# Combining-weight rows spread over partitions from on-chip memory instead of from a stored copy, and the loading loop written out

## What is computed

```python
probs = jax.nn.sigmoid(x @ router_w.T + expert_bias[None, :])
top_w, top_idx = jax.lax.top_k(probs, 8)
top_w = top_w / (jnp.sum(top_w, -1, keepdims=True) + 1e-9) * 2.5
combine = jnp.zeros((T, 160)).at[jnp.arange(T)[:, None], top_idx].set(top_w)
h1 = jax.nn.silu(jnp.einsum('th,eih->eti', x, w_gate))     # 160 experts, 64 wide
h1w = h1 * combine.T[:, :, None]
routed = jnp.einsum('eti,ehi->th', h1w, w_down)
```

## Time and profile before

| what | value |
|---|---|
| time before, median of 3 runs (lowest to highest) | 978.6 us (977.95 to 981.06) |
| the profiled execution: its own time, its span | 979.47 us, 977.4 us |
| granted TensorE clock, mean over the span | 0.997 of full |
| busy share of the span: PE, DVE, ACT, POOL | 96%, 79%, 70%, 41% |
| bytes moved by DMA, mean rate | 160.57 MB, 164 GB/s |
| HBM read, written | 105.60 MB, 2.42 MB |

### The profile page before, as it was taken

How to read it: one execution, slowest core, us unless ns; L and a number is a source line. 1 busy time by engine, 2 the same in 40 slices (tenths; PEclk the granted TensorE clock), 3 DMA queues, 4 the chain that set the end, 5 groups by cost and what they waited for, 6 DMA issues and landing times.

```text
span 977.4 us, 15761 instructions
## 1 busy us (share of the span) xinstructions
PE 940.8 (96%) x4592; PEld 684.4 (70%) x4592; DVE 770.3 (79%) x1450; ACT 681.3 (70%) x1171; POOL 402.8 (41%) x265
## 2 busy tenths in 40 slices
PE   4899999999999999999997999999999999999997
PEld 2656666666666666666543888888888888888886
DVE  5866766766676676676764999999999999999996
ACT  4656666666666666666655777877777777777775
POOL 0688888898888888898900000000000000000000
PEclk9999999999999999999999999999999999999999
DMA  7957644544553563454105999999999999999992
GB/s 217 235 161 202 166 115 103 130 100 117 130 122 78 125 152 92 104 130 101 47 18 139 224 221 220 220 219 220 218 218 220 217 219 217 221 216 220 219 218 61
DMA packets 71633, 160.57 MB, mean 164 GB/s; under 512 B 10416, under 2 KB 36336, under 8 KB 61856
## 3 DMA queue, kind: packets, MB, share of 16 engines
q1 hardware_dynamic: 70816, 158.66, 72.8%
q10 hardware_dynamic: 768, 1.31, 0.4%
HBM read 105.60 MB, written 2.42 MB: 111 GB/s over the span
## 4 chain that ended last, share of the span: by engine, by line
PE 88%; DVE 5%; ACT 3%; issue 2%; DMA 1%; POOL 1%; ACTq 0%; SPq 0%; DVEq 0%
PE ps L635 44%; PE ps L439 11%; PE ps L426 11%; PE ps L415 5%; PE ps L417 5%; PE ps L389 5%; PE ps L452 2%; PE ps L400 2%; ACT prob L729 1%; DVE prob L1032 1%; POOL prob L904 1%; DMA strips<-comb_rows 0%; DVE PT L208 0%; PE ps L374 0%; PE ps L485 0%
## 5 line engine op out<-in xcount | busy, mean ns | idle before, releaser
L904 POOL TENSOR_SCALAR prob<-prob,rinv 128x512 f32<-128x512 f32 x256 | 398.1, 1568 | 87.8 <-DVE rinv L1049 85.7
L729 ACT ACTIVATE prob<-prob,nmax 128x512 f32<-128x512 f32 x256 | 183.0, 716 | 138.7 <-DVE nmax L1032 138.6
L635 PE MATMUL ps<-hT,wT 128*128 128x512 f32 x960 | 243.9, 390 | 1.3 <-ACT oT L820 1.3
L1235 DVE TENSOR_TENSOR PT<-v_sb,strips 128x1024 f32<-128x1024 f32 x160 | 196.1, 1225 | 44.0 <-ACT v_sb L871 33.6
L871 ACT ACTIVATE v_sb<-ps 128x1024 f32<-128x1024 f32 x160 | 164.6, 1029 | 90.2 <-PE ps L635 89.9
L635 PEld LDWEIGHTS ps<-hT,wT 128*128 128x128 f32 x960 | 180.4, 188 | 40.5 <-issue 3.0
L635 PE MATMUL ps<-stack,wT 128*128 128x512 f32 x640 | 197.8, 391 | 4.3 <-DVE wT L1222 4.3
L208 DVE COPY PT<-ps 128x512 f32<-128x512 f32 x128 | 88.4, 691 | 135.4 <-PE ps L426 133.0
L1222 DVE TENSOR_TENSOR wT<-PT,stack 128x1024 fp32r<-128x1024 f32 x160 | 195.0, 1219 | 0.0
L863 ACT CAST stack<-PT 128x1024 fp32r<-128x1024 f32 x160 | 166.6, 1041 | 2.9 <-DVE PT L1235 2.9
L426 PEld LDWEIGHTS ps<-ident,prob 128*128 128x128 f32 x1024 | 114.4, 141 | 74.5 <-POOL prob L904 51.0
(11 more groups left out here) (113 smaller groups left out, 726.8 us busy)
## 6 DMA issues: line engine op xcount, KB each, us to landing
strips<-comb_rows SPq DMA_DIRECT2D x152, 512.0 KB, 12.8
stack<-qk SPq DMA_DIRECT2D x128, 256.0 KB, 3.8
k_low<-qk SPq DMA_DIRECT2D x64, 128.0 KB, 3.8
hT<-qk SPq DMA_DIRECT2D x64, 128.0 KB, 3.7
strips<-bias_rows SPq DMA_DIRECT2D x8, 896.0 KB, 5.6
strips<-in_L_ffn_w_gate SPq DMA_DIRECT2D x80, 64.0 KB, 11.2
strips<-in_L_ffn_w_down SPq DMA_DIRECT2D x80, 64.0 KB, 12.9
strips<-comb_rows SPq DMA_DIRECT2D x16, 256.0 KB, 5.7
```

The source lines that it names most:

```text
L635: last = nc.tensor.matmul(ps[:, bank + c, :], weights(a), rows(m, c), start=start and k == 0, stop=stop and k == 2, skip_group_check=True)
L729: nc.scalar.activation(prob[:, u, :], prob[:, u, :], ACT.Exp, bias=nmax[:, u:u + 1], scale=-1.0, accum_out=rsum[:, u:u + 1]).then_inc(s_ex ...
L904: nc.gpsimd.tensor_scalar(prob[:, u, :], prob[:, u, :], rinv[:, u:u + 1], None, ALU.mult).then_inc(s_prob, 1)
L1235: nc.vector.tensor_tensor(weighted[:, k % 4, :], silu[:, k % 2, :], cb[:, r, half * HALF:(half + 1) * HALF], ALU.mult).then_inc(s_mul, 1)
```

## The change

The DRAM tensor `comb_rows`, its stores and their semaphores are gone. Each row load takes its row straight from the one partition of `combT` or `combT2` that holds it, with a step of zero over the 64 destination partitions. SP waits for the copies into these tensors (`s_cev`) where it waited for the stores. The partition of the source can no longer be computed in a loop, so the loop on SP's queue is a Python loop now, and its 19 turns stand one after the other in SP's program.

```diff
-    comb_rows = nc.dram_tensor("comb_rows", [EPAIRS, 2, T], F32, kind="Internal").ap()
...
-        s_cst = [sem(f"comb_stored{b}") for b in range(B)]
...
                 for half in range(2):
-                    row = comb_rows[bass.ds(i * DEPTH + r, 1), half, tokens]
-                    sp.dma_start(cb[half * I:(half + 1) * I, r, tokens], row.broadcast_to(
-                        [I, tokens.stop - tokens.start])).then_inc(loaded or s_cb[r], 16)
+                    expert = 2 * (i * DEPTH + r) + half
+                    row = combT[expert:expert + 1, tokens] if expert < P else combT2[expert - P:expert - P + 1, tokens]
+                    count = tokens.stop - tokens.start
+                    spread = bass.AP(row.tensor, row.offset, [list(row.ap[0]), [0, I], [1, count]])
+                    sp.dma_start(cb[half * I:(half + 1) * I, r, tokens].rearrange("p (o n) -> p o n", o=1), spread.rearrange("o p n -> o p n")).then_inc(loaded or s_cb[r], 16)
...
-            sp.wait_ge(s_cst[0], 32)
-            sp.wait_ge(s_cst[1], 32)
+            sp.wait_ge(s_cev, 4)
             for r in range(2):
                 load_rows(0, r, slice(0, HALF), s_first_rows[r])
-            sp.wait_ge(s_cst[2], 32)
-            sp.wait_ge(s_cst[3], 32)
+            sp.wait_ge(s_cev, 8)
...
-            with sp.Fori(0, EPAIRS // DEPTH - 1) as i:
+            for i in range(EPAIRS // DEPTH - 1):
...
-            def store_comb(b):
-                act.wait_ge(s_cev, 2 * (b + 1))
-                act.dma_start(flat[0:P, b * S:(b + 1) * S], combT[:, b * S:(b + 1) * S]).then_inc(s_cst[b], 16)
-                act.dma_start(flat[P:E, b * S:(b + 1) * S], combT2[:, b * S:(b + 1) * S]).then_inc(s_cst[b], 16)
```

More of the change, by code:

```diff
@@ L808, in copy_comb @@
                 nc.scalar.copy(combT2[:, b * S:(b + 1) * S], ps[0:E - P, COMBS + 1, :]).then_inc(s_cev, 1)
-            flat = comb_rows.rearrange("n two t -> (n two) t")
-            def store_comb(b):
-                act.wait_ge(s_cev, 2 * (b + 1))
-                act.dma_start(flat[0:P, b * S:(b + 1) * S], combT[:, b * S:(b + 1) * S]).then_inc(s_cst[b], 16)
-                act.dma_start(flat[P:E, b * S:(b + 1) * S], combT2[:, b * S:(b + 1) * S]).then_inc(s_cst[b], 16)
             def shared_silu(n):
@@ L842, in _ @@
             copy_comb(0)
-            store_comb(0)
             sigmoids(2)
@@ L854, in _ @@
             copy_comb(1)
-            store_comb(1)
             shared_silu(0)
@@ L874, in round_of @@
                         copy_comb(3)
-                        store_comb(3)
                     if not (first and k == 0):
@@ L882, in _ @@
             copy_comb(2)
-            store_comb(2)
             shared_silu(2)
```

## The result

The changed kernel takes 3,560.8 us (median of 4 runs, 3,560.0 to 3,563.1) against 978.6 us before, a ratio of 3.63 with a 95% interval from 3.617 to 3.643. The forecast was 3,585 us. The profiled execution took 3,563.1 us with a span of 3,561.1. The runs from e3 to e11b are single executions.

What follows compares the result with a forecast made beforehand. PE set the pace in the experts, DMA barely keeping up; after the change, row loads from one partition would. Start 516.7, loads 3,050 and tail 16 give a 3,583 us span, said as 3,585 us; range 2,050 to 6,650.

Steps and rivals of the forecast that it cites:

- The price of a load: Row loads in the experts: one source partition lies behind one path of 27.5 GB/s, so 19.1 us a load.
- The sum of the loads: All row loads, counted as 160 full ones at 19.07 us each: 3,050 us, or 3,510 at 23.9 GB/s.
- The start: First row load on SP, after the second copy of batch 1: at 516.7 us instead of 519.19.
- The tail: From the last row's landing to the kernel's end: 16 us, with 1.4 us for a lower TensorE clock.
- The written-out loop: SP's queue: 11.9 us of register operations and moves go, but were hidden by waiting for VectorE, so worth nothing.
- another 0.2% of instruction loading: Larger program on SP: costed at nothing, covered by SP's waits for VectorE; without cover 2 us.
- The weights' 48 us: Weight loads from memory, 10.5 MB at 220 GB/s: up to 48 us uncovered, costed at nothing beside the row loads.
- TensorE's granted clock: Matmuls at 1.2 GHz: a round takes 43.4 us, far below 152.5, so no cost except in the tail.
- Hidden loads: Rival: one partition reads as fast as DRAM, only the stores matter, 974.5 us or 978.6; chance 0.12.
- Half a path: Rival: a single partition is slower than a path, 13.75 GB/s, 38.1 us a load, 6,636 us; slower chance 0.22.
- Two paths: Rival: loads of neighbouring experts overlap on two paths, 55 GB/s, 2,060 us if always busy; chance 0.28, all or part.
- landing times of 60 us or more: Profile of the changed kernel: row loads land after 60 us or more, with four to eight in line.

Runs made afterwards that it cites:

- e3: Changed kernel, but every row load reads partition 0, so that two paths can never work at once: 3,624.4 us.
- e11b: Changed kernel, but each row load reads the 16 partitions 0, 2, 4 to 30, each four times: 1,001.4 us.
- e1: Kernel before the change with only SP's loop written out, rows still through DRAM: 980.4 us against 979.8 beside it.
- e2: Changed kernel, but each row load copies 64 neighbouring partitions of combT once instead of one partition 64 times: 973.3 and 974.3 us.
- e4: Changed kernel, but the second row of each pair is read from a partition 64 further on, behind a different path: 3,288.4 us.
- e7: Changed kernel, but from the second round GpSimd's queue loads each pair's second row, from a partition 64 further on: 3,003.7 us.
- e8: Changed kernel, but from the second round GpSimd's queue loads each pair's second row, both rows from neighbouring partitions: 2,998.7 us.

## Why the prediction was right

**The price of a load.** The step that carried the forecast was "64 partitions are reached over half of the paths that 128 have", and that "a single partition lies behind one path". One path was put at 220 / 8 = 27.5 GB/s, a load at 19.07 us. Measured: 19.29 us (27.18 GB/s) with one path throughout (e3), 18.9 us in the changed kernel, where paths overlap a little. The sum of the loads was 3,050 us against 3,026.5 measured.

That the sum came out within 1% is in part luck, twice over. The 220 GB/s were not shown to be the limit of eight paths: by the prediction's own reading PE sets the pace there and asks for 217, a ninth of it is weights that reach all 128 partitions, and the two rows of a pair go to different halves of the partitions. That figure happens to lie near eight times what e3 measured for one path, 217. And two small misses cancel in part: at e3's rate the 160 loads would be 3,086 us, 36 more than forecast, and the overlap of paths, which the prediction put at nothing, took 60 off again.

**The start and the tail.** The loads start at 518.98 and not at 516.7: the copy that they wait for ended at 518.97 and not 516.65; why it ended later was not followed. The tail was put at 16 us and is 15.6. The written-out loop was put at nothing, and e1 confirms it. The allowance for another 0.2% of instruction loading was not needed: queue 8 carries 24 packets and 0.39 MB in the changed kernel as in the one before.

**The other costs put at nothing.** The weights' 48 us are nearly all covered. In the first round of the changed kernel no weights are in line, and a 256 KB load holds the queue for 9.59 us, with the 0.04 of issue behind it 19.26 us for a full load. e3 with all its weights has 19.29, so about 5 of the 48 us are left at most. TensorE's granted clock averaged 0.59 of full from 1,000 to 2,000 us, after waits for ScalarE of 30 us each (2,275.9 us in 76). It stood at 0.50, the level of 1.2 GHz, in 18 of the 26 stretches of 3 us that follow 2,000 us, and PE is still busy only about a fifth of the time.

**The rivals.** Hidden loads: wrong for one partition, right for 64 (e2, 973.3 to 974.3 us, as the 974.5 worked out for it). Half a path: wrong. Two paths: the overlap exists, and gives 2% in the changed kernel, 8% in e4, 16% with two queues. My reason against it, that all engines start on the same row, was wrong: in e4's first round one queue keeps two paths full (54 GB/s). What saved the forecast is the order of the experts, four neighbouring rows behind one path, so that the path changes only with every fourth row load. What holds the overlap down in the later rounds of e4, e7 and e8 stays open.

**What I read wrongly.** I expected landing times of 60 us or more and VectorE's wait for rows as the longest. SP's queue takes no more than about two loads ahead (34.2 us to landing at 18.9 us a load) and then holds SP in the issue itself. So the line never gets four pairs deep, the chain is 83% SP's queue and 1% DMA, and ScalarE's wait for weights queued behind rows is the longest. None of this moves the time, because the path is busy all along. The first multiplication came at 540.5 and not 536 us.

## What to carry to other kernels

A transfer is priced on both of its sides: count over how many groups of partitions it reads as well as over how many it writes, since one partition read 64 times gives 27 GB/s even with all 16 DMA engines at work on it. A row that was to be spread over partitions again and again was better off in DRAM here, where the same 64 readings kept up 220 GB/s. Saving 4 us of stores is no bargain when it moves 84 MB of readings behind one path: look at what the store bought before removing it. If rows must come from SBUF, neighbouring loads should lie behind different paths.

## What the runs showed of the hardware that I had not expected

- SP's queue is held inside the issue of a transfer when the loads ahead have not moved: 9.59 us for each 256 KB load, 15 to 18 us for a 64 KB weight load behind two row loads. Such time appears in the chain under the queue's name and not under DMA.
- One queue's loads can use two paths at once: 54 GB/s in e4's first round, where neighbours lie behind different paths and only row loads are in line. With larger loads and weights between the pairs it was 34 GB/s, and a second queue brought 38 to 39. The Trainium skill, "DMA: Bandwidth & Descriptors", section on issuing engines, says that issuing on several engines only saves the sequencer's issue time; here it also took the changed kernel from 3,561 to 2,999 us, because it let a second path work.
- Eight paths read, always the same ones, gave 205 GB/s (e11b). Reading 64 partitions, the lower and the upper half in turn, kept up with PE at 222 GB/s (e2).
